# A graph network in one program: one addition and one attribute load moved to other engines, and the edge order changed

## The chip, the core and the metric

The kernel runs as one program on one core of a Trainium2 chip. The metric is the device time of one execution in microseconds (us), and for comparisons the median over several executions. The engines are TensorE (PE in the profile, with PEld for its weight loads), VectorE (DVE), ScalarE (ACT), GpSimd (POOL) and SyncE (SP). Each runs its own list of instructions in order and waits on semaphores. DMAs are issued from SP, ACT and POOL; gathers and scatters by index, and DMAs that add to their target, are issued from POOL here.

## What is computed

Two graph layers over 100,000 nodes with 64 features and 25,000 edges, sorted by destination. All is float32.

```python
h = relu(layernorm(x))
# layer 0
a = softmax over the edges of one dst of sum(h[src] * h[dst])
agg = segment_sum((h @ W_conv + b_conv)[src] * a, dst)
out = agg + relu(h @ W_res + b_res)
x2 = x + batchnorm_over_nodes(out)
# layer 1
h2 = relu(layernorm(x2))
m = gelu(gelu([h2[src], h2[dst], edge_attr] @ W_m1 + b_m1) @ W_m2 + b_m2)
boxes = segment_sum(m, dst)
c = gelu([h2, boxes] @ W_c1 + b_c1)
result = x2 + h2 + gelu(c @ W_c2 + b_c2)
```

## The kernel before

Nodes are worked on in 49 steps (S) of 128 partitions with 16 rows each, so a step's tile is 128 x 1024. Edges are worked on in 49 groups (G) of 512: 4 edges (EJ) on each of 128 partitions. The order of everything is written out by hand, as loops over pairs of steps or groups, one loop per engine. There are three stages.

The **first stage** computes layer 0 for nodes and edges at once. POOL gathers the rows of x for source and destination of every edge (8 gathers of 128 rows for a group, L587), groups in falling order. VectorE subtracts means, scales, and scans segments; TensorE transposes and multiplies; each group ends with its rows of agg, kept in SBUF. Then follow the batch norm's sums. During this stage POOL also begins to scatter agg rows to the table agg_rows in DRAM (put_agg, 4 scatters a group, L591).

The **node stage** makes x2, h2 and the result of layer 1 for all nodes as if boxes were zero. For a step s VectorE adds the normed r product to x (L937), subtracts the mean (L764, L766), sums squares (L756), inverts the deviation for two steps together (L694 to L702) and scales (L770), which gives h2 in the tile xc. POOL then adds h2 to x2 (add_h2, L637). TensorE transposes h2 (L1335) and makes both products (L1456, L1466), ScalarE the gelus, and VectorE adds the result (final_rows, L949), which SP stores. There are CS = 3 buffers of xc: x2_center of step s waits for the addition of step s - 3. In POOL's list the additions stand between the scatters of agg, and, once all 49 groups are scattered, between gathers of agg rows for the edges' sources (gather_agg, 4 a group, L587). How many groups stand in the list up to step s is `agg_groups(s)`. A gathered group goes to one of RS = 4 buffers, agg_ring, and SP stores it to edge_agg in DRAM (stash_agg, L521).

The **edge stage** corrects the rows of nodes that have edges. For a group g SP loads the edges' r product to rr[g % 6] (load_edges, L499). POOL adds the gathered agg of the source with an adding DMA from edge_agg (add_agg, L625, 128 x 256), VectorE multiplies by the batch norm's scale (scale_r, L981), and POOL adds x with another adding DMA (add_x, L631, 128 x 512). TensorE sums this with the filled agg of the destination (sum_edges, L1516 and L1519), VectorE makes h2 again (edge_x2, edge_h2), and transposes (L1530), the message products (L1540, L1542, L1549), a scan on VectorE (L1016), the last products (L1556, L1567), a transpose back (L1578) and edge_final (L1024) follow. A pair of groups is one turn of each engine's loop, in which stages of earlier groups are also worked on. SP's turn is: load_edges, load_prev (the masks for the scans), load_attr (the attributes; it waits for the message product that read the buffer before, C_m1), stash_agg. POOL's list has, for each g, add_agg(g + 2), add_x(g), the gather of a later group while there is one, and scatters of final rows (put_final, 4 a group, L591):

```python
ahead = agg_groups(S - 1) - G
last = G - ahead
...
due = min(g - 9, 2 * (g - last))
```

So no final row is scattered before group `last`, then two groups of them for every g, until they are 9 groups behind.

Edge 4p + j of a group lies on partition p in column j. After a transpose its place is column 4p + j of 512, so that in PSUM and in the weights of L1519 and L1367 every fourth column is addressed (`j:p*EJ:EJ`), 16 bytes apart.

## Time and profile before

| what | us |
|---|---|
| median of 3 executions | 1741.92 |
| their lowest and highest | 1740.9, 1746.1 |
| span of the profiled execution | 1753.3 |

The profiled execution is 11.4 us longer than the median. Its parts are: the first stage with its batch norm to about 656 us, the node stage to about 1166 us, where POOL's first add_agg stands, and the edge stage to the end. A busy engine is not always the bound, and for PE the busy time is modelled. A "wait" of 0.3 us for "issue" stands before nearly every gather and scatter of POOL and belongs to its cost.

### The profile page before, as it was taken

The numbers are of one execution on the slowest core, as the hardware profiler recorded it, in microseconds if no ns is written. First come the engines' busy times: TensorE is split into PE (matmuls) and PEld (weight loads), VectorE is DVE, ScalarE is ACT, GpSimd is POOL, SyncE is SP. The second block draws the span as 40 slices with busy tenths as digits, with TensorE's granted clock in tenths as the row PEclk, the third lists the DMA queues.
The fourth block names the chain that finished last, engine by engine and source line by source line (L and its number), as shares of the span: only waits on it lengthen the run. The fifth ranks groups of instructions, "written<-read, shape, count | busy, mean of one in ns | idle before, by whom it ended". The sixth has DMA issues, their size and how long they took to land.

```text
span 1753.3 us, 21724 instructions
## 1 busy us (share of the span) xinstructions
PE 1375.6 (78%) x6521; PEld 942.1 (54%) x6521; DVE 1361.7 (78%) x2229; ACT 833.2 (48%) x1448; POOL 1363.7 (78%) x1135
## 2 busy tenths in 40 slices
PE   3487777777776776988999889858889988787993
PEld 1266666666555564766667666634445444343541
DVE  8899899989877858898889888825767766555871
ACT  4655455545543435776668666621333432332441
POOL 7777777778777778788888887675767768888676
PEclk9788889888887877898889888955888987886987
DMA  7788776545543363444545565545656554545520
GB/s 210 249 283 290 282 264 219 165 145 157 161 150 96 106 224 102 157 166 166 201 162 186 174 200 178 160 98 108 121 120 124 118 117 97 107 89 98 122 48 18
DMA packets 154342, 273.55 MB, mean 156 GB/s; under 512 B 58386, under 2 KB 69361, under 8 KB 154228
## 3 DMA queue, kind: packets, MB, share of 16 engines
q1 hardware_dynamic: 71144, 183.91, 31.1%
q0 software_dynamic: 68112, 49.85, 16.7%
q10 hardware_dynamic: 14972, 38.41, 5.9%
q8 instruction: 54, 0.88, 0.2%
q14 instruction: 60, 0.49, 0.1%
HBM read 151.68 MB, written 121.80 MB: 156 GB/s over the span
## 4 chain that ended last, share of the span: by engine, by line
POOL 40%; issue 20%; DVE 18%; PE 13%; DMA 6%; ACT 2%; SPq 0%; POOLq 0%; DVEq 0%; ACTq 0%
POOL agg_rows L591 11%; POOL out L591 10%; POOL agg_ring L587 7%; DVE stat L756 4%; POOL xt L637 3%; DVE stat L764 3%; POOL part L587 3%; DMA rr<-edge_x 3%; DMA edge_agg<-agg_ring 2%; POOL rr L631 2%; DVE xc L770 1%; PE banks L1350 1%; DVE sums L821 1%; PE banks L1542 1%; PE banks L1540 1%
## 5 line engine op out<-in xcount | busy, mean ns | idle before, releaser
L587 POOL DMA_INDIRECT agg_ring<-agg_rows,edge_idx x196 | 233.2, 1190 | 112.2 <-DMA edge_agg<-agg_ring 57.2
L591 POOL DMA_INDIRECT agg_rows<-agg,put_first x196 | 234.0, 1194 | 55.9 <-issue 54.7
L587 POOL DMA_INDIRECT part<-in_x,edge_idx x192 | 217.3, 1132 | 58.5 <-issue 58.2
L591 POOL DMA_INDIRECT out<-agg,put_last x196 | 212.0, 1082 | 59.6 <-issue 59.6
L1335 PE MATMUL banks<-ident,xc 128*128 128x128 f32 (+1 forms) x784 | 135.1, 322 | 141.6 <-DVE xc L770 140.9
L1466 PEld LDWEIGHTS banks<-packed,cT 97*128 97x128 f32 (+1 forms) x1568 | 210.4, 218 | 45.3 <-issue 44.3
L1466 PE MATMUL banks<-packed,cT 97*128 97x64 f32 (+1 forms) x1568 | 218.6, 303 | 0.5 <-ACT cT L1198 0.5
L1335 PEld LDWEIGHTS banks<-ident,xc 128*128 128x128 f32 (+1 forms) x784 | 113.3, 177 | 152.0 <-DVE xc L770 130.8
L1456 PE MATMUL banks<-hT,packed 64*96 64x512 f32 (+1 forms) x392 | 125.5, 718 | 47.6 <-ACT cT L1198 43.0
L1081 ACT ACTIVATE hT<-banks 128x512 f32<-128x512 f32 (+1 forms) x98 | 55.4, 595 | 205.7 <-PE banks L1335 204.3
L587 POOL DMA_INDIRECT x_ring<-in_x,edge_idx x104 | 121.4, 1167 | 34.2 <-issue 34.2
L1516 PE MATMUL banks<-rr,ident 128*128 128x512 f32 (+1 forms) x98 | 69.2, 795 | 86.7 <-DMA rr<-edge_x 86.7
L587 POOL DMA_INDIRECT gout<-in_x,edge_idx x96 | 111.3, 1159 | 29.3 <-issue 29.3
L981 DVE TENSOR_TENSOR rr<-rr,bn 128x512 f32<-128x512 f32 (+1 forms) x49 | 33.9, 692 | 122.0 <-DMA rr<-edge_agg 122.0
L756 DVE TENSOR_REDUCE stat<-sq 128x16 f32<-128x1024 f32 (+1 forms) x98 | 117.1, 1212 | 14.6 <-ACT sq L1073 14.6
L1073 ACT ACTIVATE sq<-xc 128x1024 f32<-128x1024 f32 (+1 forms) x98 | 102.9, 1050 | 52.6 <-DVE xc L766 52.3
L1350 PE MATMUL banks<-hT,packed 128*128 128x512 f32 (+1 forms) x196 | 119.1, 739 | 1.3 <-ACT hT L1081 1.3
L766 DVE SCALAR_TENSOR_TENSOR xc<-stat,xt 128x1024 f32<-128x1024 f32 (+1 forms) x86 | 117.6, 1368 | 3.0
L770 DVE SCALAR_TENSOR_TENSOR xc<-xc,stat 128x1024 f32<-128x1024 f32 (+1 forms) x98 | 117.1, 1217 | 1.7
L1519 PEld LDWEIGHTS banks<-fill_b,sums 65*128 65x128 f32 (+1 forms) x392 | 99.0, 326 | 32.0 <-issue 19.1
L764 DVE TENSOR_REDUCE stat<-xt 128x16 f32<-128x1024 f32 (+1 forms) x86 | 104.1, 1210 | 14.3 <-POOL xt L637 6.1
L1257 ACT ACTIVATE sq<-banks 128x512 f32<-128x512 f32 (+1 forms) x49 | 28.9, 590 | 177.0 <-PE banks L1530 173.2
(163 smaller groups left out, 3351.2 us busy)
## 6 DMA issues: line engine op xcount, KB each, us to landing
xt<-in_x SPq DMA_DIRECT2D x84, 512.0 KB, 5.2
r_rows<-rT ACTq DMA_DIRECT2D x48, 512.0 KB, 5.4
agg_rows<-rb SPq DMA_DIRECT2D x48, 512.0 KB
out<-xt SPq DMA_DIRECT2D x36, 512.0 KB, 3.0
edge_r<-rr ACTq DMA_DIRECT2D x48, 256.0 KB, 5.0
rT<-r_rows SPq DMA_DIRECT2D x24, 512.0 KB, 6.5
part<-r_rows SPq DMA_DIRECT2D x24, 512.0 KB, 6.9
rr<-edge_r SPq DMA_DIRECT2D x48, 256.0 KB, 3.2
```

Source lines behind the costliest of these rows:

```text
L587: A.indirect_dma_start(to, None, table[:, :], bass.IndirectOffsetOnAxis(ap=idx, axis=0), bounds_check=limit, oob_is_err=False).then_inc(si ...
L591: A.indirect_dma_start(table[:, :], bass.IndirectOffsetOnAxis(ap=idx, axis=0), rows_of, None, bounds_check=limit, oob_is_err=False).then_i ...
L756: V.tensor_reduce(total, rows(squares), AX, ALU.add).then_inc(st.sem, 1)
L764: V.tensor_reduce(total, rows(source), AX, ALU.add).then_inc(st.sem, 1)
L766: V.scalar_tensor_tensor(out=rows(tile), in0=per_row(total), scalar=-1.0 / D, in1=rows(source), op0=ALU.mult, op1=ALU.add).then_inc(st.sem, 1)
L770: V.scalar_tensor_tensor(out=tile, in0=source, scalar=0.0, in1=per_row(deviation), op0=ALU.max, op1=ALU.mult).then_inc(st.sem, 1)
L1073: A.activation(sq[s % 2][0:p, :], xc[s % CS][0:p, :], ACT.Square).then_inc(st.sem, 1)
L1335: ins = T.transpose(to[:, c:c + p], xc[s % CS][0:p, c:c + P], ident[0:p, 0:p])
L1350: T.matmul(blocks(W[0][:, c], p), wres2[:, :], blocks(hT[:, c], p), start=True, stop=True)\
L1456: ins = T.matmul(blocks(bank(4 + i)[0:H2, :], p), wc1_node[i * D:i * D + D, :], blocks(hT[i * D:i * D + D, b * HALF:(b + 1) * HALF], p), s ...
L1466: ins = T.matmul(to[0:p, i * D:i * D + D], cT[b][:, i % 2, (i // 2) * P:(i // 2) * P + p], wc2[:, :], start=(i == 0), stop=(i == 7))
L1519: ins = T.matmul(to[:, j * P:(j + 1) * P], fillT[g % 2][0:D + 1, j:p * EJ:EJ], fill_b[:, :], start=False, stop=(j == EJ - 1))
```

## The change

Four things are changed.

1. In the node stage the additions of h2 to x2 for odd steps move from POOL to VectorE (add_h2_here, right after x2_center of the next even step). POOL keeps the even ones. `agg_groups` is larger, so that 83 instead of 75 groups of scatters and gathers stand in POOL's list of the node stage; `ahead` is 34 instead of 26 and `last` 15 instead of 23.
2. In the edge stage the gathered agg is loaded by SP to a ring of 4 new tiles (agg_in), and VectorE adds it in scale_r. POOL's add_agg is gone.
3. The attributes of group g + 4 are loaded by a DMA in ScalarE's list, behind the gelu of group g. SP loads only the first four.
4. Edge j * 128 + p of a group lies on partition p, column j. The index table is laid out so, and all addresses `j:p*EJ:EJ` become `j*p:(j+1)*p`.

```diff
+MI = 4
+        agg_in = [sb(f"agg_in{q}", [P, EW]) for q in range(MI)]
...
         def agg_groups(s):
-            return PUTS_AHEAD + s + 1 + (s + 1) // 6
+            return PUTS_AHEAD + 4 * (s + 1) // 3
...
+            def load_agg(g):
+                C_ra.part(sp, g - MI, 1)
+                p = edges_of(g)
+                sp.wait_ge(Y_st.of(g), Y_st.after(g))
+                sp.dma_start(agg_in[g % MI][0:p, :], edge_agg[g][0:p, :]).then_inc(C_ga.of(g), 16)
...
-                for g, do in ((a + 6, load_edges), (a + 7, load_edges), (a + 4, load_prev), (a + 5, load_prev),
-                              (a + 4, load_attr), (a + 5, load_attr)):
+                for g, do in ((a + 4, load_agg), (a + 6, load_edges), (a + 5, load_agg), (a + 7, load_edges),
+                              (a + 4, load_prev), (a + 5, load_prev)):
...
             for s in range(S):
-                add_h2(s)
+                if s % 2 == 0:
+                    add_h2(s)
...
-            for g in range(2):
-                add_agg(g)
             for g in range(G):
-                if is_group(g + 2):
-                    add_agg(g + 2)
                 add_x(g)
...
+            def add_h2_here(s):
+                p = nodes_of(s)
+                here = xb[s % XB][0:p, :]
+                B_h.done(dve, s)
+                V.tensor_tensor(here, here, xc[s % CS][0:p, :], ALU.add).then_inc(B_yv.sem, 1)
...
                 if a in pair:
                     x2_center(a)
+                if is_step(a - 1):
+                    add_h2_here(a - 1)
                 if is_step(a - 3):
                     final_rows(a - 3)
...
                 here = rows(rr[g % 6][0:p, :])
+                to = side(rr[g % 6][0:p, :], 1)
+                dve.wait_ge(C_ld.of(g), C_ld.after(g))
                 dve.wait_ge(C_ga.of(g), C_ga.after(g))
+                V.tensor_tensor(to, to, rows(agg_in[g % MI][0:p, :]), ALU.add).then_inc(C_ra.sem, 1)
+                dve.wait_ge(C_ra.sem, C_ra.after(g, 1))
                 V.tensor_tensor(here, here, cols(bn[0:p, 0, :], ER), ALU.mult).then_inc(C_ra.sem, 1)
...
                 A.activation(m1T[g % 2][0:H1, 0:c], bank(5)[0:H1, 0:c], ACT.Gelu, bias=bm1[:, :]).then_inc(C_g1.sem, 1)
+                if is_group(g + 4):
+                    load_attr(g + 4)
...
-                    ins = T.matmul(to[:, j * P:(j + 1) * P], fillT[g % 2][0:D + 1, j:p * EJ:EJ], fill_b[:, :],
+                    ins = T.matmul(to[:, j * P:(j + 1) * P], fillT[g % 2][0:D + 1, j * p:(j + 1) * p], fill_b[:, :],
...
-    idx[:, :, :G - 1] = four[:, :main].reshape(4, G - 1, P, EJ).transpose(2, 0, 1, 3)
+    idx[:, :, :G - 1] = four[:, :main].reshape(4, G - 1, EJ, P).transpose(3, 0, 1, 2)
```

POOL's list at the end of the node stage and the start of the edge stage, before (L637 is the addition of h2, L587 a gather of agg rows, L625 add_agg, L631 add_x):

```order
L637 TENSOR_TENSOR part<-part,xc 128x1024
L584 REGISTER_ALU
L587 DMA agg_ring<-agg_rows,edge_idx 128x64 x4
L584 REGISTER_ALU
L587 DMA agg_ring<-agg_rows,edge_idx 128x64 x4
L637 TENSOR_TENSOR xt<-xt,xc 106x1024
L584 REGISTER_ALU
L587 DMA agg_ring<-agg_rows,edge_idx 128x64 x4
L625 DMA rr<-edge_agg 128x4x64 x3
L631 DMA rr<-edge_x 128x512
L584 REGISTER_ALU
L587 DMA agg_ring<-agg_rows,edge_idx 128x64 x4
```

and now (L644 is the addition, L601 the gather, L638 add_x):

```order
L644 TENSOR_TENSOR part<-part,xc 128x1024
L598 REGISTER_ALU
L601 DMA agg_ring<-agg_rows,edge_idx 128x64 x4
L598 REGISTER_ALU
L601 DMA agg_ring<-agg_rows,edge_idx 128x64 x4
L598 REGISTER_ALU
L601 DMA agg_ring<-agg_rows,edge_idx 128x64 x4
L644 TENSOR_TENSOR xt<-xt,xc 106x1024
L598 REGISTER_ALU
L601 DMA agg_ring<-agg_rows,edge_idx 128x64 x4
L638 DMA rr<-edge_x 128x512
L598 REGISTER_ALU
```

Three groups stand between two additions where one or two stood, and add_x follows the last gather with no add_agg ahead of it.

SP's turn of the edge stage, before (L499 is load_edges, L426 load_prev, L505 load_attr, L521 stash_agg):

```order
L499 DMA rr<-edge_r 128x512 x2
L426 DMA xc<-prev_row 128x512 x2
L505 DMA attr<-in_edge_attr_t 32x512 x2
L521 DMA edge_agg<-agg_ring 128x256 x2
L499 DMA rr<-edge_r 128x512 x2
```

and now (L512 is load_agg, L506 load_edges, L433 load_prev, L534 stash_agg):

```order
L512 DMA agg_in<-edge_agg 128x256
L506 DMA rr<-edge_r 128x512
L512 DMA agg_in<-edge_agg 128x256
L506 DMA rr<-edge_r 128x512
L433 DMA xc<-prev_row 128x512 x2
L534 DMA edge_agg<-agg_ring 128x256 x2
```

The attribute loads, which waited for a message product, no longer stand ahead of the stores of the gathered agg.

## Rows read from the trace of the kernel before

**Rows 1.** The page: span, and the chain that ended last, by engine.

```profile
span 1753.3 us, 21724 instructions
...
POOL 40%; issue 20%; DVE 18%; PE 13%; DMA 6%; ACT 2%; SPq 0%; POOLq 0%; DVEq 0%; ACTq 0%
```

**Rows 2.** Busy time by stretch: length, then each engine's us (and instructions), clock, DMA.

```profile
0.00:606.00 606.00, 423.44 (x2126) 342.67 (x2126) 534.23 (x957) 305.06 (x603) 477.31 (x420) 0.85 0.61 200
...
678.00:1166.00 488.00, 434.54 (x2704) 323.09 (x2704) 412.64 (x503) 317.94 (x480) 402.02 (x279) 0.86 0.49 166
1166.00:1412.00 246.00, 202.07 (x640) 105.94 (x641) 163.29 (x298) 74.57 (x131) 163.01 (x144) 0.80 0.62 121
```

**Rows 3.** Waits of POOL over the whole span: total us, times, longest.

```profile
POOL agg_ring L587 <- DMA edge_agg<-agg_ring: 57.2, 9, 15.3
```

**Rows 4.** POOL's groups of instructions, 678 to 1166: busy, mean ns, idle before.

```profile
L591 POOL DMA_INDIRECT agg_rows<-agg,put_first x125 | 153.1, 1224 | 34.3 <-issue 33.7
L587 POOL DMA_INDIRECT agg_ring<-agg_rows,edge_idx x104 | 128.3, 1233 | 40.9 <-issue 27.1 <-DMA edge_agg<-agg_ring 13.1
L637 POOL TENSOR_TENSOR xt<-xt,xc 128x1024 f32<-128x1024 f32 x36 | 90.1, 2502 | 9.8 <-DVE xc L770 9.3
```

**Rows 5.** VectorE's groups of instructions, 680 to 1165.

```profile
L949 DVE TENSOR_TENSOR xt<-xt,gout 128x1024 f32<-128x1024 f32 x36 | 57.5, 1598 | 2.8 <-ACT gout L1206 2.8
...
L766 DVE SCALAR_TENSOR_TENSOR xc<-stat,xt 128x1024 f32<-128x1024 f32 x33 | 51.9, 1573 | 1.1
...
L937 DVE TENSOR_TENSOR xt<-banks,xt 128x1024 f32<-128x1024 f32 x32 | 39.0, 1218 | 12.7 <-PE banks L1438 12.7
```

**Rows 6.** POOL's groups of instructions, 1166 to 1753.

```profile
L591 POOL DMA_INDIRECT out<-agg,put_last x196 | 212.0, 1082 | 59.6 <-issue 59.6
L587 POOL DMA_INDIRECT agg_ring<-agg_rows,edge_idx x92 | 104.9, 1140 | 71.2 <-DMA edge_agg<-agg_ring 44.1 <-issue 27.1
L631 POOL DMA_DIRECT2D rr<-edge_x x49 | 68.5, 1397 | 5.4 <-DVE rr L981 5.4
L625 POOL DMA_DIRECT2D rr<-edge_agg x49 | 67.4, 1405 | 17.6 <-DMA rr<-edge_r 17.6
```

**Rows 7.** Timeline, start us and length: two message products one pair of groups apart.

```profile
1637.23 1.09 PE L1542 MATMUL banks<-sq,packed 128*80 128x512 f32 x2
...
1653.84 1.08 PE L1542 MATMUL banks<-sq,packed 128*80 128x512 f32 x2
```

**Rows 8.** Busy time in exactly that pair, columns as in rows 2.

```profile
1637.23:1653.84 16.61, 16.61 (x62) 8.72 (x61) 14.74 (x28) 7.45 (x13) 13.31 (x13) 1.00 0.66 133
```

**Rows 9.** Timeline where POOL scatters two groups for each add_x.

```profile
1489.58 2.00 PE L1542 MATMUL banks<-sq,packed 128*80 128x512 f32 x2
...
1502.53 1.40 POOL L631 DMA_DIRECT2D rr<-edge_x  x1
...
1515.69 1.40 POOL L631 DMA_DIRECT2D rr<-edge_x  x1
```

**Rows 10.** Timeline: the first scale_r, add_x of group 4, add_x of group 48.

```profile
1173.82 0.69 DVE L981 TENSOR_TENSOR rr<-rr,bn 128x512 f32<-128x512 f32 x1 [7.12 <-DMA rr<-edge_agg]
...
1205.50 1.43 POOL L631 DMA_DIRECT2D rr<-edge_x  x1
...
1683.41 1.05 POOL L631 DMA_DIRECT2D rr<-edge_x  x1
```

**Rows 11.** Timeline of TensorE: eight instructions with adjacent, then with spaced weight columns.

```profile
304.43 1.05 PE L1385 MATMUL banks<-packed,heT 128*128 128x128 f32 x8
...
305.54 1.87 PE L1367 MATMUL banks<-packed,sums 65*128 65x65 f32 x8
...
307.24 0.60 PE L1358 MATMUL banks<-ident,weighted 128*65 128x128 f32 x4
```

**Rows 12.** Mean ns by line: a transpose with spaced, one with adjacent PSUM columns.

```profile
L1504 PE MATMUL banks<-ident,agg 128*64 128x128 f32 x192 | 37.6, 331 | 0.0
L1376 PE MATMUL banks<-ident,part 128*128 128x128 f32 x192 | 37.0, 327 | 3.3 <-DVE part L770 3.3
```

More of the change, by code:

```diff
@@ L281, in program @@
         B_h = stage("h2_ready")
-        B_y = stage("h2_added_to_x2")
+        B_y = stage("h2_added_on_gpsimd")
+        B_yv = stage("h2_added_on_vector")
         B_t = stage("h2_transposed", 2)
@@ L292, in program @@
         C_ld = Slots(E_st.sems, before=G)
-        C_ga = slots("gathered_agg_added", 4)
+        C_ga = slots("gathered_agg_loaded", MI)
         C_x = slots("edge_x_added", 4)
@@ L298, in program @@
         C_fs = stage("agg_filled")
-        C_ra = stage("edge_r_scaled")
+        C_ra = stage("edge_r_scaled", 2)
         C_as = stage("edge_x2_summed")
@@ L513, in load_prev @@
                     sp.wait_ge(B_t.sem, B_t.after(S - 1))
-                    sp.wait_ge(B_y.sem, B_y.after(S - 1))
+                    h2_added(sp, S - 1)
+                    h2_added(sp, S - 2)
                 load_same(mask[g % MS], prev_row, g, g, 0, P, C_sm)
@@ L542, in _ @@
                             load_attr(g)
+                            load_agg(g)
                         load_edges(g)
@@ L619, in gather_agg @@
                     gather(agg_ring[g % RS][0:p, j * D:(j + 1) * D], agg_rows, idx_of(src_idx, g, j, p), G_a.of(g))
-            def add_agg(g):
-                p = edges_of(g)
-                pool.wait_ge(C_ld.of(g), C_ld.after(g))
-                pool.wait_ge(Y_st.of(g), Y_st.after(g))
-                A.dma_start(side(rr[g % 6][0:p, :], 1), rows(edge_agg[g][0:p, :]), accum_op=ALU.add)\
-                 .then_inc(C_ga.of(g), 16)
             def add_x(g):
@@ L947, in final_rows @@
                 dve.wait_ge(B_og.sem, B_og.after(s))
-                dve.wait_ge(B_y.sem, B_y.after(s))
+                h2_added(dve, s)
                 V.tensor_tensor(here, here, gout[s % 2][0:p, :], ALU.add).then_inc(B_fin.sem, 1)
@@ L1262, in copy_dst_x2, with load_attr @@
                 A.activation(rows(agg_of(g, p)), side(bank(1 + g % 2)[0:p, :], 0), ACT.Copy).then_inc(C_xd.sem, 1)
+            def load_attr(g):
+                C_m1.done(act, g - 4)
+                c = edges_of(g) * EJ
+                q = (g % 4) * DE
+                A.dma_start(attr[q:q + DE, 0:c], eaT[:, g * EG:g * EG + c]).then_inc(C_ea.of(g), 16)
             def edge_gelu1(g):
@@ L1670, in edge_layout @@
     main = (G - 1) * EG
-    idx[:, :, :G - 1] = four[:, :main].reshape(4, G - 1, P, EJ).transpose(2, 0, 1, 3)
-    rest = four[:, main:E].reshape(4, -1, EJ)
-    idx[:rest.shape[1], :, G - 1] = rest.transpose(1, 0, 2)
+    idx[:, :, :G - 1] = four[:, :main].reshape(4, G - 1, EJ, P).transpose(3, 0, 1, 2)
+    rest = four[:, main:E].reshape(4, EJ, -1)
+    idx[:rest.shape[2], :, G - 1] = rest.transpose(2, 0, 1)
     windows = np.stack([pad[k:E + k].reshape(FP, FC) for k in range(3)], axis=1)
```

16 lines of the change are left out of this document (9 added, 7 removed).

## The prediction, made blind

> **What bounds the kernel now.** I read the chain that ended last first [rows 1]: POOL and the "issue" gaps, which are mostly POOL's 0.3 us ahead of each gather or scatter, make 60% of it. No engine is far behind, so the question is the same in each stage: which list is never idle?
>
> In the first stage VectorE is busy 534 of 606 us, POOL 477 plus 0.3 us for each of its 420 instructions, together about 600 [rows 2]. POOL is gapless, and the stage ends with its last gathers.
>
> In the node stage POOL has 229 indirect DMAs. With the gap ahead of each they take (153.1 + 34.3 + 128.3 + 27.1) / 229 = 1.50 us each [rows 4]. 228 of them, with 49 additions of 2.5 us, make 342 + 122 = 464 of 488 us. The other 24 us are its waits, 13.1 for the agg ring and about 10 for h2 [rows 4]. So POOL's list sets this stage, but VectorE (413) and TensorE (435) stand close behind it [rows 2].
>
> In the edge stage the length goes by pairs of groups. From add_x of group 4 to that of group 48 there are 22 pairs in 1683.4 - 1205.5 = 477.9 us, 21.7 each [rows 10]. A clean pair takes 16.61 us, with TensorE busy all of it and VectorE 14.74 [rows 7, 8]. The difference comes from two things. While POOL still gathers, it stands 57.2 us in 9 waits, 44.1 of it here, for the store that frees a buffer of agg_ring [rows 3, 6]. SP issues this store behind the attribute load, which waits for a message product. Later POOL scatters two groups for each add_x, and two add_x are 1515.69 - 1502.53 = 13.2 us apart, 26.3 a pair [rows 9]. After the last add_x come 1753.3 - 1683.4 = 69.9 us, in which POOL has 44 scatters of 1.39 left [rows 6]: 61 us, so the tail is POOL's as well.
>
> **First stage: 1 us less.** Only the addresses change. TensorE loads weights for L1367 from spaced columns. Eight instructions take 1.87 us, and eight of L1385 with adjacent ones 1.05 [rows 11], so 0.8 us a group go. POOL and VectorE set this stage and TensorE waits for them, so this shows only for the last groups, behind the last gather. I take 1 us (0 to 3).
>
> **Node stage: 7 us less.** POOL's list changes from 228 indirect DMAs and 49 additions to 260 and 25: 390 + 62 = 452 us, 12 less. VectorE gets 24 additions. Both inputs lie in SBUF, as in L949, which without a stretch takes as long as L937, 1.22 us: 29 us. But L949 and L766 are stretched to 1.60 and 1.57 [rows 5], and the candidates for it are POOL's additions. (0.38 + 0.35) x 48 = 35 us for 49 additions are 0.71 each, and 24 of them go: 17 back. VectorE's net 12 us fit into the 75 us that it is idle. In the other direction, POOL's indirect DMAs take 1.22 to 1.23 us here [rows 4] and 1.08 where fewer large VectorE operations run [rows 6]. 0.14 x 228 = 32 us over 147 such VectorE operations are 0.22 each, so 24 more cost POOL 5. That leaves 7. Bounds: 20 less, if its waits shrink too; 12 more, if VectorE's net addition lies wholly on the path. In VectorE's list x2_center of the next odd step and two final additions are queued behind add_h2_here. It waits for nothing there, since h2 is VectorE's own result of the turn before.
>
> The Trainium skill (GPSIMD Engine Reference, Key points) says that GpSimd shares its SBUF interfaces with VectorE and is disturbed by VectorE instructions with two SBUF inputs; by it, the new additions in either stage would cost POOL time, as the 5 us above do.
>
> **Start of the edge stage: 9 us less.** The first scale_r waits 7.1 us for the adding DMA of POOL [rows 10], which stands behind POOL's last gathers. Now agg_in is loaded while the node stage runs, and scale_r follows the last final addition at once: 7 less. The first groups also come sooner by one DMA issue of 1.4 us each on POOL; two of these I count, 2 us.
>
> **The 22 pairs: 85 us less.** Each engine's need for a pair:
>
> - TensorE: 16.6 in the clean pair, less 2 x 0.8 for the weights of L1519: 15.0.
> - VectorE: 14.74 and two additions of 128 x 256. Half of the 0.69 that 128 x 512 takes [rows 10] to two thirds of it, 0.45: 15.6. The clean pair has 1.9 us in which VectorE waits for ScalarE's squares or for its own last result. The new work can fill little of that, so 17.2. Ends: 16.6 (all of it filled) and 19.2 (2 us of new waiting).
> - POOL while it gathers: 8 x 1.43 + 2 x (1.40 + 0.3) = 14.9. Without add_agg it loses 2 x 1.4 us and its waits for rr. With one group of scatters for each g: 8 x 1.39 + 3.4 = 14.5.
>
> So VectorE takes POOL's place as the bound, with 17.2. The stall on agg_ring goes: stash_agg now stands behind loads that wait for sum_edges and message_scan of earlier turns, a pair ahead of the product that it waited for. What is late next is POOL's double scattering. From `last` = 15 on, 2 * (g - last) overtakes g - 9 after six groups, where it took 14 before. In these three pairs POOL needs 16 x 1.39 + 3.4 = 25.6. It falls behind by 3 x (25.6 - 17.2) = 25 us. TensorE wants an add_x only in the next pair, so a part is absorbed. I take 15 (0 to 25).
>
> Sum: 22 x 17.2 + 15 = 393, against 478: 85 less. The DMAs of the attributes cost ScalarE an issue and no more, since it is busy 7.5 of 16.6 us [rows 8]. The tail of 69.9 us stays, since as many scatters are left behind the last add_x.
>
> On addresses, the two transposes that write PSUM with 16 bytes between columns (L1504) or without (L1376) take 331 and 327 ns [rows 12], so I count nothing for those. The Trainium skill (SBUF — State Buffer, Door 1: The DMA port swizzle) has two rules here. Any non-contiguous access to PSUM significantly slows matmuls, so the transposes would get faster, on an engine that no longer bounds. And a stride of four fp32 in SBUF is free, so L1519 would gain nothing and TensorE would stay at 16.6 a pair, below 17.2, with the same sum. Rows 11 and 12 disagree with both.
>
> **The sum.** 1 + 7 + 9 + 85 = 102 us off the profiled execution's 1753.3: 1651. That execution is 11.4 us above the median, and I take the same difference from the median: 1741.9 - 102 = 1640.
>
> **The rivals.**
>
> *Waits remain in the pairs.* VectorE, TensorE and ScalarE hand over to each other several times a pair, and the clean pair shows this loop only with TensorE as its pace. If VectorE as the pace leaves 19.2 a pair, the pairs take 22 x 19.2 + 15 = 437, 41 less instead of 85: 1684. For it: the many waits for ScalarE; a low clock in places has the same effect. Against: a clean pair appears wherever POOL keeps up. Chance 0.22.
>
> *All goes well.* Pairs at 16.6, the double scattering absorbed, and the node stage 20 shorter: 113 + 20 + 9 + 3 = 145 less, 1597. Near this, below 1605: 0.08.
>
> *TensorE's clock falls, and it ends slower.* In the clean pair the clock is 2.4 GHz (1.00) [rows 8]. At 1.2 GHz the two passes of L1542 take 2.00 instead of 1.09 us [rows 7, 9]. Once TensorE waits for VectorE in every pair, as it waits in the stretches with 0.80 [rows 2], it might be given the low level for most of the stage. At the low level a pair needs 15.0 x 1.8 = 27. This decides if the pair passes 21.7 + 17/22 = 22.5, that is if TensorE spends over 60% of its work at 1.2 GHz; at 85% the pair is 25.2 and the time 1742 + 77 - 17 = 1802. Against: a TensorE that has become the bound doesn't idle, and the dense stretch has the full clock. Chance 0.04.
>
> *The change doesn't do what it says.* agg_in could come late, because load_agg stands in SP's list between load_edges, which wait for sum_edges; then one DMA wait is only replaced by another, and with pairs of 21.7 the time is 1742 - 7, or within 0.3% if the node stage gives nothing. SP reaches it a pair early, so 0.04 together, 0.03 of it within 0.3%.
>
> **How the numbers follow.** The forecast, 1605 to 1665, has 0.62, the rivals 0.22, 0.08, 0.04 and 0.04. The range 1605 to 1695 leaves out the last two, the best case and the upper end of the first rival. Faster by over 0.3% (5 us, about what a measurement of this kernel can tell from no change): 0.93; within it 0.03; slower 0.04.
>
> **What would show it.** VectorE's wait ahead of scale_r, and POOL's for agg_ring in the edge stage, near zero; add_x of groups 4 to 48 in about 393 us; three pairs of about 25 from group 16; L1519 and L1367 at about 1.05 us for eight at full clock; L949's mean below 1.5; first add_x about 7 us sooner after the last node rows. I am wrong if VectorE is idle over 3 us a pair in the edge stage, if the node stage gets longer, or if the granted clock there falls below 0.7.

## The result, and the profile after

| | us |
|---|---|
| median before, 4 executions | 1741.7 (1740.9 to 1746.1) |
| median after, 4 executions | 1619.6 (1614.9 to 1620.4) |
| ratio, 95% interval | 0.9295 (0.9271 to 0.9318) |
| predicted | 1640 (1605 to 1695) |

It is faster by 122 us, 20 more than predicted, and inside the range. The profiled executions lie further apart than the medians: 1753.3 before, 11.4 above its median [rows 1], 1613.1 after, 6.5 below its own. So the terms below add up to 140 us, and 18 of them are scatter between executions. This scatter favoured the forecast: between the two profiled executions the miss is 38 us, between the medians 20.

The page of the changed kernel, span and chain by engine; [rows 1] had POOL at 40%:

```profile
span 1613.1 us, 21823 instructions
...
POOL 31%; DVE 28%; issue 19%; PE 13%; DMA 4%; ACT 3%; DVEq 0%; SPq 0%; POOLq 0%; ACTq 0%
```

The stages can be laid beside each other by four marks: POOL's first and last addition of h2, and its add_x of groups 4 and 48. From the timeline of after (start us, length):

```profile
675.95 2.35 POOL L644 TENSOR_TENSOR xt<-xt,xc 128x1024 f32<-128x1024 f32 x1
...
1148.72 2.36 POOL L644 TENSOR_TENSOR xt<-xt,xc 106x1024 f32<-106x1024 f32 x1
...
1191.35 1.02 POOL L638 DMA_DIRECT2D rr<-edge_x  x1
...
1544.10 1.00 POOL L638 DMA_DIRECT2D rr<-edge_x  x1 [1.08 <-DVE rr L997]
```

and the first two marks in before (its last two are in [rows 10]):

```profile
678.34 2.38 POOL L637 TENSOR_TENSOR xt<-xt,xc 128x1024 f32<-128x1024 f32 x1
...
1158.12 2.36 POOL L637 TENSOR_TENSOR xt<-xt,xc 106x1024 f32<-106x1024 f32 x1
```

| stretch | before | after | difference | predicted |
|---|---|---|---|---|
| to the first addition of h2 | 678.3 | 676.0 | -2.4 | -1 |
| to the last (node stage) | 479.8 | 472.8 | -7.0 | -7 |
| to the add_x of group 4 | 47.4 | 42.6 | -4.8 | -9 |
| to the add_x of group 48, 22 pairs | 477.9 | 352.8 | -125.1 | -85 |
| tail | 69.9 | 69.0 | -0.9 | 0 |

Nearly the whole of the surprise is in the pairs. The two message products one pair apart, and busy time in exactly that pair and in a longer stretch of the steady part (columns as in [rows 2]; [rows 7, 8] are before's):

```profile
1412.36 1.08 PE L1566 MATMUL banks<-sq,packed 128*80 128x512 f32 x2
...
1428.36 1.08 PE L1566 MATMUL banks<-sq,packed 128*80 128x512 f32 x2
```

```profile
1412.36:1428.36 16.00, 15.09 (x61) 6.62 (x61) 15.32 (x30) 7.45 (x13) 11.51 (x11) 1.00 0.55 143
...
1364.00:1544.00 180.00, 169.62 (x672) 74.18 (x672) 172.48 (x326) 84.39 (x149) 133.74 (x119) 1.00 0.56 135
```

A steady pair is 16.0 us, not 17.2. VectorE is busy 15.32 of it, and over 180 us 96%; TensorE has 15.09. VectorE is the pace, as forecast. Two of POOL's waits over the whole execution, which answer [rows 3]:

```profile
POOL rr L638 <- DVE rr L997: 32.6, 22, 7.1
POOL agg_ring L601 <- DMA edge_agg<-agg_ring: 21.8, 8, 7.9
```

POOL now waits for VectorE's scale_r. Of the 21.8 us for the ring, 17.0 lie in the node stage and only 4.8 in the edge stage, where there were 44.1 [rows 6]. The double scattering is still there. POOL's three pairs from add_x 16 take 23.4, 24.9 and 23.7 us, as forecast (about 25), and two pairs at the message products 20.6 and 23.5 us:

```profile
1304.83 1.08 PE L1566 MATMUL banks<-sq,packed 128*80 128x512 f32 x2
...
1325.44 1.08 PE L1566 MATMUL banks<-sq,packed 128*80 128x512 f32 x2
...
1348.89 1.09 PE L1566 MATMUL banks<-sq,packed 128*80 128x512 f32 x2
```

### The profile page after: what moved, and what is told of

The parts are those of the page before. It is cut to its first block, busy times and chain, and to the rows that moved or that the text cites. A ratio compares the mean times of both kernels' runs of the same rounds, so it can differ in the third digit from the quotient of the medians.

```text
span 1613.1 us, 21823 instructions
## 1 busy us (share of the span) xinstructions
PE 1254.2 (78%) x6521; PEld 842.9 (52%) x6521; DVE 1376.9 (85%) x2302; ACT 832.7 (52%) x1448; POOL 1250.2 (78%) x1062
## 2 busy tenths in 40 slices
DMA packets 132612, 273.54 MB, mean 170 GB/s; under 512 B 30404, under 2 KB 47658, under 8 KB 132496
## 4 chain that ended last, share of the span: by engine, by line
POOL 31%; DVE 28%; issue 19%; PE 13%; DMA 4%; ACT 3%; DVEq 0%; SPq 0%; POOLq 0%; ACTq 0%
POOL agg_rows L605 12%; POOL part L601 6%; DVE stat L760 4%; DVE stat L768 4%; POOL out L605 4%; PE banks L1490 3%; POOL agg_ring L601 3%; DVE sq L1032 3%; DVE part L774 2%; DVE sums L1006 2%; POOL gout L601 2%; POOL x_ring L601 2%; DMA edge_agg<-agg_ring 2%; PE banks L1480 2%; PE banks L1374 2%
## 5 line engine op out<-in xcount | busy, mean ns | idle before, releaser
L601 POOL DMA_INDIRECT agg_ring<-agg_rows,edge_idx x196 | 233.7, 1192 | 82.8 <-issue 55.9
L605 POOL DMA_INDIRECT out<-agg,put_last x196 | 221.7, 1131 | 59.8 <-issue 59.5
L601 POOL DMA_INDIRECT part<-in_x,edge_idx x192 | 218.9, 1140 | 58.5 <-issue 57.6
L1490 PEld LDWEIGHTS banks<-packed,cT 97*128 97x128 f32 (+1 forms) x1568 | 214.7, 222 | 42.6 <-issue 42.4
L1490 PE MATMUL banks<-packed,cT 97*128 97x64 f32 (+1 forms) x1568 | 223.0, 307 | 0.0
L601 POOL DMA_INDIRECT x_ring<-in_x,edge_idx x104 | 122.0, 1173 | 34.3 <-issue 34.0
L601 POOL DMA_INDIRECT gout<-in_x,edge_idx x96 | 109.1, 1137 | 29.3 <-issue 28.7
L760 DVE TENSOR_REDUCE stat<-sq 128x16 f32<-128x1024 f32 (+1 forms) x98 | 117.2, 1212 | 16.6 <-ACT sq L1089 16.6
L768 DVE TENSOR_REDUCE stat<-xt 128x16 f32<-128x1024 f32 (+1 forms) x86 | 104.1, 1210 | 19.6 <-POOL xt L644 14.6
L770 DVE SCALAR_TENSOR_TENSOR xc<-stat,xt 128x1024 f32<-128x1024 f32 (+1 forms) x86 | 111.9, 1302 | 2.9
L1213 ACT ACTIVATE cT<-banks,packed 96x512 f32<-96x512 f32 (+1 forms) x98 | 66.8, 681 | 71.8 <-PE banks L1480 71.6
L1382 PE MATMUL banks<-ident,weighted 128*65 128x128 f32 (+1 forms) x196 | 36.7, 321 | 75.0 <-DVE weighted L815 75.0
L1222 ACT ACTIVATE gout<-banks 128x512 f32<-128x512 f32 (+1 forms) x98 | 57.7, 589 | 59.9 <-PE banks L1490 59.9
L1127 ACT ACTIVATE esq<-part 128x512 f32<-128x512 f32 (+1 forms) x98 | 61.2, 625 | 48.6 <-DVE part L770 48.6
```

Source lines behind the costliest of these rows:

```text
L601: A.indirect_dma_start(to, None, table[:, :], bass.IndirectOffsetOnAxis(ap=idx, axis=0), bounds_check=limit, oob_is_err=False).then_inc(si ...
L605: A.indirect_dma_start(table[:, :], bass.IndirectOffsetOnAxis(ap=idx, axis=0), rows_of, None, bounds_check=limit, oob_is_err=False).then_i ...
L760: V.tensor_reduce(total, rows(squares), AX, ALU.add).then_inc(st.sem, 1)
L768: V.tensor_reduce(total, rows(source), AX, ALU.add).then_inc(st.sem, 1)
L770: V.scalar_tensor_tensor(out=rows(tile), in0=per_row(total), scalar=-1.0 / D, in1=rows(source), op0=ALU.mult, op1=ALU.add).then_inc(st.sem, 1)
L1213: A.activation(blocks(cT[b][0:H2, 0, :], p), blocks(bank(4)[0:H2, :], p), ACT.Gelu, bias=bc1[:, :])
```

## Experiments on one part at a time

The first four kernels ran on one chip beside before, which took 1743.2 us there (median of 7). They are compared with after's 1619.6.

**Part 2 taken back.** GpSimd adds the gathered agg again; VectorE only scales. The other parts of the change stay.

```diff
-                            load_agg(g)
...
-                V.tensor_tensor(to, to, rows(agg_in[g % MI][0:p, :]), ALU.add).then_inc(C_ra.sem, 1)
...
+                if is_group(g + 2):
+                    add_agg(g + 2)
                 add_x(g)
```

> The changed kernel with one part undone: POOL adds the gathered agg again with an adding DMA, and VectorE has no addition in scale_r. The rest stays (fewer gathers in the edge stage, attributes from ScalarE, new edge order). Theory: VectorE paces the clean pairs of the changed kernel at 16.0 us, but POOL needs 2 x 1.4 us more a pair, about 17.3 while it gathers and 16.9 to 17.3 with one group of scatters, and 28 in the three pairs with two groups. So the pairs come out at about 17.3, which is 22 x 1.3 + 8 = 37 us more than the changed kernel, plus 5 for the first scale_r: 1660. Rival (the adding DMA was never the cost, only the ring stalls were): VectorE loses 0.9 us of work a pair and the time stays within 8 us of 1620.

Measured: 1638.8 us (1635.8 to 1640.6), 0.940 of before (0.937 to 0.943). That is 19 more than after, half of what the theory said. GpSimd, 124 us of the steady part, its groups and then all engines:

```profile
L598 POOL DMA_INDIRECT out<-agg,put_last x65 | 66.7, 1026 | 19.7 <-issue 19.7
L638 POOL DMA_DIRECT2D rr<-edge_x x17 | 24.2, 1422 | 0.0
L632 POOL DMA_DIRECT2D rr<-edge_agg x16 | 23.6, 1475 | 0.0
```

```profile
1436.00:1560.00 124.00, 123.76 (x489) 53.65 (x488) 114.86 (x215) 62.29 (x110) 104.60 (x98) 1.00 0.70 134
```

GpSimd is busy for 104.6 us of the 124, and 19.7 us of issue gaps fill it up; a pair takes 15.06. TensorE is filled too, 123.76 of 124 us at full clock, and 15.06 is also the 15.1 us that its work of a pair takes. So GpSimd keeps up here, and which of the two sets the pair the trace doesn't part. It is faster than after's 16.0, where VectorE is the pace: in this part of the edge stage moving the addition cost 0.9 us a pair. It pays elsewhere, by the time that the two adding DMAs take in GpSimd's list. They overlap in the profile:

```profile
1519.62 1.33 POOL L632 DMA_DIRECT2D rr<-edge_agg  x1
1520.46 1.39 POOL L638 DMA_DIRECT2D rr<-edge_x  x1
```

That is 2.2 us for both, not the sum of their lengths, and only the 1.0 of add_x is left in after: 1.2 us less for each group. The way from add_x 4 to 48 is 369.2 us against 352.8. To group 16, while GpSimd still gathers, it is 5.3 us longer; in the six steps with two groups of scatters, 13.1 to 14.6 us each for 11.5 to 13.0, it is 9.5 longer. Behind them it is 1.6 longer in all: the shorter steady pairs only make up for a late one at the end (20.5 us). The way from the last addition of h2 to add_x 4 is 4.4 us longer (47.0 against 42.6), so the gain at the start of the edge stage belongs to this part.

**Part 3 taken back.** SP loads the attributes, at the end of its turn ahead of the stash, as before the change. Part 2 stays, so SP has load_agg as well.

```diff
             def load_attr(g):
+                C_m1.done(sp, g - 4)
...
-                              (a + 4, load_prev), (a + 5, load_prev)):
+                              (a + 4, load_prev), (a + 5, load_prev), (a + 4, load_attr), (a + 5, load_attr)):
...
-                if is_group(g + 4):
-                    load_attr(g + 4)
```

> The changed kernel with one part undone: SP loads the attributes again, at the end of its turn and ahead of the stores of gathered agg. Theory: the store that frees agg_ring and load_agg come one pair later again. While POOL gathers (15 groups, 7 pairs) this costs about 6 us every second pair, 15 to 25 us; in the rest SP loads agg_in for group a + 4 only after the message product of group a + 1, and scale_r of a + 4 would wait for it: 1 to 4 us a pair more in 15 pairs. Together 30 to 60 us more: 1650 to 1680. Rival: the loads are early enough anyway and only the ring stall returns: 10 to 20 us more, 1630 to 1640.

Measured: 1792.3 us (1788.3 to 1794.7), 1.027 of before (1.023 to 1.030). Both expectations missed by over 110 us. This kernel is slower than before, and the waits tell why (total us, times, longest), of SP's own list, of VectorE and of POOL:

```profile
SPq L518 <- PE banks L1559: 474.1, 45, 19.5
```

```profile
DVE rr L996 <- DMA agg_in<-edge_agg: 190.6, 22, 14.9
```

```profile
POOL rr L639 <- DVE rr L998: 151.7, 28, 12.5
POOL agg_ring L602 <- DMA edge_agg<-agg_ring: 72.6, 13, 18.2
```

SP stands at load_attr until the message product (L1559 here) has read the old attributes. The agg_in load of the next turn is queued behind that. I read these waits so: the product of one pair releases SP, SP starts agg_in, VectorE adds it, and only then can the next products come, a closed loop of 24 us a pair. In before the wait was there too, 427.7 us, but behind it stood only loads with a lead of two turns and the stash. With SP's turn in this order, part 3 is a precondition of part 2.

**Part 3 alone, put into before.**

```diff
-                              (a + 4, load_attr), (a + 5, load_attr)):
+                              ):
...
+                if is_group(g + 4):
+                    load_attr(g + 4)
```

> The kernel before with one part of the change alone: the attributes of group g + 4 are loaded from ScalarE's list. Theory: SP's stores of gathered agg come a pair earlier, and the 44 us of waits for agg_ring in the edge stage and the 18 for rr go. In the part with gathers POOL then needs 8 x 1.43 + 2 x 3.1 = 17.7 a pair instead of about 20.4, over 11 pairs 30 us; the part with two scattered groups for each g stays at 26.3 a pair. Time 1742 - 30 to 45 = 1697 to 1712. Rival: the ring stalls only took the place of waits for TensorE, 0 to 10 us less.

Measured: 1693.9 us (1693.6 to 1695.6), 0.972 of before (0.968 to 0.975). So this one edit brings 49 us of the 122, a little more than the 30 to 45 expected. POOL's wait for the ring:

```profile
POOL agg_ring L586 <- DMA edge_agg<-agg_ring: 13.4, 5, 7.9
```

against 57.2 [rows 3], 44 us less. The pairs while POOL gathers are 16.6 us; while it scatters twice they stay at 26.3.

**Part 4 taken back.** Edge 4p + j lies on partition p again.

```diff
-T.matmul(to[:, j * P:(j + 1) * P], fillT[g % 2][0:D + 1, j * p:(j + 1) * p], fill_b[:, :],
+T.matmul(to[:, j * P:(j + 1) * P], fillT[g % 2][0:D + 1, j:p * EJ:EJ], fill_b[:, :],
```

and so in the other five places and in the index tables.

> The changed kernel with one part undone: edge 4p + j on partition p again, with columns 16 bytes apart in PSUM and in the weights. Theory: VectorE paces a pair at 16.0, TensorE needs 15.1 and with the old weight loads 16.6 to 16.8. So TensorE becomes the bound by 0.6 to 0.8 us a pair, 13 to 18 us, and the last groups of the first stage cost 1 to 3: 14 to 20 us more, 1634 to 1640. Rival, by my prediction, in which VectorE needed 17.2: no change, within 5 us of 1620.

Measured: 1640.6 us (1630.0 to 1645.5), 0.940 of before (0.935 to 0.945), 21 more than after. TensorE's message products in its steady part:

```profile
1417.35 1.09 PE L1566 MATMUL banks<-sq,packed 128*80 128x512 f32 x2
...
1433.95 1.09 PE L1566 MATMUL banks<-sq,packed 128*80 128x512 f32 x2
```

The pair is 16.61 us, the same as the clean pair of before [rows 7]: TensorE bounds it, at full clock, and VectorE's two additions are hidden. The way from add_x 4 to 48 is 370.0 us, 17 of the 21. The sum of parts: 49 us for part 3 alone, 19 for part 2 and 21 for part 4 when each is the last to come. The remaining 33 show in none of these four runs. Part 1, the moved additions of h2 with the larger table, wasn't taken back here, and the rest is what the parts bring only together; such a sum needn't close, since part 3 was measured without the others and they with it.

**VectorE's time, made longer.** A dummy addition of 128 x 256, read by nobody, goes in behind each scale_r; the outputs are unchanged. This run and the next three had another chip, on which before takes 1948.7 us (median of 11, 1899.2 to 1970.1; the section on the hardware says what is other there). In the next experiment, whose edge stage is that of after, steady pairs take 16.0 us there too, so the edge stage can be compared between the chips; whole times only within one.

```diff
+                C_ra.done(dve, g - 1)
+                V.tensor_tensor(prod[:, :], packed[:, 0:EW], packed[:, EW:2 * EW], ALU.add).then_inc(C_ra.sem, 1)
```

> The kernel after with one dummy VectorE addition (128x256, its result read by nobody) put into each group of the edge stage, behind scale_r. In the steady pair of after VectorE is busy 15.32 us of 16.0 and has no wait that its trace shows. Theory (VectorE alone sets the pair, and every us of work on it counts in full): two additions of 0.42 us and their gaps make the steady pair 16.9 us; over 22 pairs, 4 or 5 of them set by the scatters of two groups a turn, 17 x 0.9 = 15 to 20 us, so 1635 to 1640. Rival (VectorE still waits for others somewhere in the pair, and fills that time): pair 16.0 to 16.3, 1620 to 1627.

Measured: from add_x 4 to 48 371.2 us. The kernel of the next experiment took 353.0 on this chip: 18.2 more, as the theory said. (Whole time: 1869.9, 1856.4 to 1880.9; the numbers near 1635 were for the first chip.) Two pairs of its steady part:

```profile
1697.73:1731.86 34.13, 31.87 (x121) 14.09 (x120) 32.35 (x63) 14.89 (x26) 20.93 (x20) 0.95 0.53 130
```

A pair is 17.06 us with VectorE busy 16.18: 0.86 more work, 1.06 more time, idle 0.88 a pair where after has 0.68. VectorE's list is the pace. TensorE's granted clock was 0.95 in this window, where it was 1.00 in after's, and whether the other 0.2 us come from that the run doesn't show.

**h2 all on GpSimd.** The order of the indirect DMAs stays as in after.

```diff
-                if s % 2 == 0:
-                    add_h2(s)
+                add_h2(s)
...
-                if is_step(a - 1):
-                    add_h2_here(a - 1)
```

> The kernel after with all 49 additions of h2 on GpSimd again; the number of indirect DMAs in the node stage (83 groups), and all of the edge stage, as in after. Theory (what the node stage of before was short of is GpSimd's time, and VectorE's additions buy it): 24 additions of 2.50 us return to an engine that is busy 382 us of the 481 from first to last addition, and they hold up the chain x2 to h2 to relu, so the node stage grows by 20 to 55 us: 1640 to 1675. Rival (GpSimd has 99 us to spare there and the additions run in it): 1612 to 1628.

Measured: 1841.7 us (1836.5 to 1868.5); the kernel with the spread scatters below, which has half of these additions on VectorE, took 1837.6. The node stages, this kernel first, then the other:

```profile
858.00:1372.00 514.00, 449.31 (x2688) 332.17 (x2688) 419.88 (x507) 321.03 (x481) 422.10 (x305) 0.83 0.49 162
```

```profile
853.00:1369.00 516.00, 446.19 (x2638) 331.61 (x2640) 415.03 (x529) 318.74 (x473) 374.62 (x280) 0.82 0.49 160
```

GpSimd does 47 us more in the same time. Its waits for VectorE in either, this kernel's first:

```profile
POOL xt L644 <- DVE xc L773: 106.9, 3, 104.7
...
POOL part L644 <- DVE xc L773: 1.1, 1, 1.1
```

```profile
POOL xt L644 <- DVE xc L774: 26.6, 6, 9.6
POOL part L644 <- DVE xc L774: 20.9, 4, 6.6
```

The 104.7 us are the wait ahead of the stage's first addition, which isn't in the other kernel's list: that one is taken from 858 us on, behind its first addition; without it this kernel waits 3.3 us and goes through, where the other waits 47.5. So on this chip the rival holds. This list has no slack left, though: 422.1 us busy, 69.8 of issue gaps, 17.4 of waits for DMAs and the 3.3 make 513 of 514 us. In the first trace of after GpSimd has no such wait: 376.4 us busy, 72.4 of issue gaps and 22.0 of waits for DMAs make 471 of the 473 us. I ran it once more beside after, to see it on a chip like the first:

> The kernel after with all 49 additions of h2 on GpSimd. On the other chip its node stage took 513.5 us, GpSimd going through it without a gap (422 us busy, 70 of issue, 20 of waits for DMAs), and the kernels with half of the additions took 516 to 519 with GpSimd waiting 47 us for VectorE. In the first trace of after GpSimd has no such wait and needs 473 us (376 busy, 72 issue, 22 for DMAs). Theory (on a chip where the node stage runs as in that trace GpSimd sets it, and the moved additions are worth their time): 513 us against 473, so 35 to 40 us slower than after, 1655 to 1660. Rival (the stage is set by TensorE's clock, as on the other chip, and where the additions stand is worth nothing): within 5 us of after.

> The kernel after, unchanged, beside the three others. The runs with dummy additions, with all h2 on GpSimd, with fewer indirects and with spread scatters were timed on a chip where the kernel before takes 1948.7 us, not 1742, so what they cost or gain can be read only stage by stage; this is the missing ratio. Expected: 0.930 of before and 353 us from the add_x of group 4 to that of group 48 if the chip is like the first one; if it is like the other, about 0.948 of before and the same 353 us, since the run with all h2 on GpSimd, whose edge stage is that of after, showed 353.0 there.

But that chip was like the second (before 1988.7 us, 1961.2 to 2005.8). This kernel took 1892.3 us (1858.5 to 1911.6), after 1898.0 (1843.6 to 1910.3), 0.954 of before by the medians and 0.940 by the lowest of each. Four executions that scatter by 3% show no difference between this kernel and after. The node stage took 521.1 and 544.1 us in profiled executions 40 and 49 us above the lowest of their kernels. From add_x 4 to 48 the same code took 355.2 and 359.8 us there, where two other traces had 352.8 and 353.0; why, I can't explain. What the move of h2 is worth on the first chip stays open. The sum of GpSimd's list says up to 40 us; no run shows it.

**Fewer indirects in the node stage.** The table of the node stage is that of before (75 groups, not 83).

```diff
-            return PUTS_AHEAD + 4 * (s + 1) // 3
+            return PUTS_AHEAD + s + 1 + (s + 1) // 6
```

> The kernel after with the old table of the node stage: 75 groups of indirect DMAs beside the additions of h2, not 83, so 8 groups (32 DMAs) go back to the edge stage and its scatters begin at group 23, not 15. Theory (GpSimd doesn't set the node stage any more, TensorE and VectorE do, so taking 40 us of work from it gives little, and the edge stage has too few scatter turns left): node stage shorter by 5 to 20 us, edge stage longer by 15 to 35 us, since two groups a turn last longer; 1628 to 1645. Rival (the node stage is still set by GpSimd, so its 32 x 1.24 = 40 us return there, and the edge stage hides them): node stage -30 to -40, edge stage +0 to +10, 1585 to 1600.

Measured: 1855.8 us (1849.1 to 1869.6). The kernel with all of h2 on GpSimd, 14 us below it, is the nearest on this chip with the larger table, and after itself didn't run there. The node stage is 492.7 us, 24 to 27 shorter than in the two kernels there whose node stage is that of after (516.5 and 519.5), and the way from add_x 4 to 48 is 390.8, 38 longer than the 353.0. The theory had the direction of both, and both are somewhat larger than it said (5 to 20 and 15 to 35). 14 add_x in a row have two groups of scatters between them, and five pairs take 23.6 to 26.8 us. The rival had hoped for 30 to 40 us in the node stage and for a cover in the edge stage. An indirect DMA costs 0.8 us in the node stage (25 / 32), and 1.2 where it is left to the edge stage (38 / 32), so the larger table is a gain, of some 13 us by these two stretches. That the stage gets shorter at all, though GpSimd waits 47.5 us for VectorE in the kernel with the larger table, no run explains.

**The scatters spread.** One number of after.

```diff
-                due = min(g - 9, 2 * (g - last))
+                due = min(g - 9, 6 * (g - last) // 5)
```

> The kernel after with one number changed: put_final begins at the same group 15 but takes 6 groups in 5 turns, not 2 a turn until it has caught up, so no turn but every fifth has two. In after two pairs there took 20.6 and 23.5 us for 16.0. By the groups of GpSimd in a steady pair (8 indirects of 1.17 us with 0.3 us of issue each, 2 additions of 0.97) a pair with 2.4 groups needs 14.8 us, under VectorE's 16.0. Theory: the bump goes and nothing takes its place, -9 to -12 us, 1608 to 1611. Rival (the scatters are then late at the end and are waited for there, or slow every fifth turn): within 4 us of after, or up to 5 slower, 1616 to 1625.

> The kernel after with put_final taking 6 groups in 5 turns, beside after on one chip: on the other chip the way from the add_x of group 4 to that of group 48 took 344.0 us, 9 less than the 353 of after's code there. Expected now 344 and 9 to 10 us less than after in the median (0.5 to 0.6%); a rival is that the tail behind group 48 takes the gain back, then less than 4.

Measured: the way from add_x 4 to 48 takes 344.0 us the first time and 343.7 the second, against 353.0 and 352.8 for after's edge stage. All pairs from group 4 to 42 are 16.0 to 16.7 us in both; the bump is gone. The first and the last mark on the second chip:

```profile
1423.39 1.02 POOL L638 DMA_DIRECT2D rr<-edge_x  x1
...
1767.43 1.04 POOL L638 DMA_DIRECT2D rr<-edge_x  x1
```

The whole times are 1837.6 us (1823.2 to 1859.5), 0.943 of before's median there, and 1855.0 (1850.3 to 1884.9), 0.937 of before (0.925 to 0.949), where after took 1898.0 (1843.6 to 1910.3), its lowest below all of these. The tail behind add_x 48 is 71.0 and 75.4 us, for after's 69.0 and 69.4. So the 9 us are seen twice between the two marks; in whole times they are smaller than the scatter of these chips, and a gain over after isn't established.

**The additions of agg split.** On top of the spread scatters, from group 18 on GpSimd adds agg for odd groups and VectorE for even ones.

```diff
+def by_pool(g):
+    return g >= 18 and g % 2 == 1
...
+                if is_group(g + 2) and by_pool(g + 2):
+                    add_agg(g + 2)
                 add_x(g)
```

> The kernel after with the scatters spread (6 groups in 5 turns from group 15) and, from group 18 on, the gathered agg of every odd group added by GpSimd's adding DMA, that of the even ones still by VectorE. A pair then costs VectorE 15.6 us (16.0 less one addition of 0.42), GpSimd 14.8 on average with 2.4 groups of scatters and one more adding DMA of 1.0 + 0.3, so 16.1 where a pair has 12 indirects and 13.6 where it has 8. Theory (VectorE and TensorE set the pair, each by its own sum of work; TensorE needs 15.1): 12 to 15 pairs of 15.5 to 15.7, so 5 us less than with the scatters spread alone, 14 less than after. Rival (GpSimd's turns with two groups of scatters set the pace of every fifth turn and what is won in the others is lost there): within 3 us of the spread scatters alone, or up to 10 slower.

Measured: 1889.8 us (1888.2 to 1894.0), 0.956 of before (0.946 to 0.965), and 363.2 us from add_x 4 to 48, 19 more than with the spread scatters alone. The theory fell, and the rival named the place but not the size. Message products of its steady part:

```profile
1660.92 1.08 PE L1592 MATMUL banks<-sq,packed 128*80 128x512 f32 x2
...
1685.39 1.08 PE L1592 MATMUL banks<-sq,packed 128*80 128x512 f32 x2
...
1700.22 1.08 PE L1592 MATMUL banks<-sq,packed 128*80 128x512 f32 x2
```

One pair takes 24.5, the next 14.8. GpSimd's groups from 1645 to 1800 fill the window, with 26.1 us of issue:

```profile
L617 POOL DMA_INDIRECT out<-agg,put_last x86 | 101.9, 1184 | 26.1 <-issue 26.1
L657 POOL DMA_DIRECT2D rr<-edge_x x17 | 20.9, 1232 | 0.0
L651 POOL DMA_DIRECT2D rr<-edge_agg x9 | 12.1, 1349 | 0.0
```

My 14.8 us for an average pair was too low even without the adding DMA: 9.6 x (1.17 + 0.3) + 2 x 0.97 = 16.1, and in the trace of the spread scatters GpSimd used 15.4 of 16.0 (124.6 us busy and 29.1 of issue gaps in 160). With the adding DMA one of the two groups takes 2.25 us for both DMAs, and GpSimd needs 9.6 x (1.18 + 0.30) + 2.25 + 1.0 = 17.5 us. The way from add_x 20 to 40 is 17.5 us a pair. The list that had been relieved became the bound again.

## Why the prediction was right

**What bounds.** In the edge stage VectorE takes GpSimd's place: right, and shown by the dummy additions, since each us of VectorE's work there costs about a us. That GpSimd's list sets the first two stages fits its trace, where it has hardly a gap, but no run tests it for the first stage, and for the node stage the one test that told something, on the second chip, went to the rival.

**First stage, 1 us: 2.4**, inside 0 to 3, but not by the cause that was named. The kernel before with part 3 alone, which keeps the old addresses, has its first addition of h2 at 675.9 us, and after with the old addresses at 676.7, where the three kernels with the new ones have 675.8 to 676.4. So the addresses show next to nothing here, and the 2.4 us are for the most part scatter of before's profiled execution.

**Node stage, 7 us: 7.0.** That it agrees so well is luck. The same node stage as in before, in the kernel with part 3 alone, lasts from the first to the last of these:

```profile
675.92 2.37 POOL L636 TENSOR_TENSOR xt<-xt,xc 128x1024 f32<-128x1024 f32 x1
...
1151.77 2.36 POOL L636 TENSOR_TENSOR xt<-xt,xc 106x1024 f32<-106x1024 f32 x1
```

475.9 us, not 479.8. That of after takes 472.8, and 473.3, 475.6 and 475.3 with one of the other parts taken back. By these six traces the change brings 0.3 to 7 us here, with 32 more indirect DMAs done in the stage; GpSimd's list itself (busy and issue) went from 454 to 449 us. The stretch of VectorE by GpSimd's additions went as worked out. The rows of after that answer [rows 5]:

```profile
L959 DVE TENSOR_TENSOR xt<-xt,gout 128x1024 f32<-128x1024 f32 x36 | 48.1, 1336 | 0.0
L770 DVE SCALAR_TENSOR_TENSOR xc<-stat,xt 128x1024 f32<-128x1024 f32 (+1 forms) x34 | 47.5, 1398 | 1.2
```

1598 became 1336 and 1573 became 1398 ns. GpSimd's indirect DMAs took 1241 and 1237 ns for 1224 and 1233 [rows 4], 3 us in all where I had said 5.

**Start of the edge stage, 9 us: 4.8.** The wait of 7.1 us [rows 10] is gone, and VectorE adds and scales at once:

```profile
1158.49 1.23 DVE L959 TENSOR_TENSOR xt<-xt,gout 106x1024 f32<-106x1024 f32 x1 [10.83 <-ACT gout L1222]
1159.63 0.42 DVE L995 TENSOR_TENSOR rr<-rr,agg_in 128x256 f32<-128x256 f32 x1
1160.08 0.69 DVE L997 TENSOR_TENSOR rr<-rr,bn 128x512 f32<-128x512 f32 x1
```

But what ends last there is the last final_rows, which waits 10.8 us for ScalarE; the gathers behind the last h2 were no longer what the first scale_r stood behind. The 2 us for an issue less on POOL were 0.4: from add_x 0 to 4 it took 30.7 us before and 30.3 after.

**The 22 pairs, 85 us: 125.** This is the term that was mis-sized. TensorE's need of 15.0 us is 15.1. For VectorE I had 15.6 of work, and it has 15.3. The step that failed is the idle time: of 1.9 us in the clean pair I let the new work fill only 0.3, because VectorE waits there for ScalarE's squares. The end "16.6 (all of it filled)" was the nearest, and even that kept TensorE's old pace. Those waits were slack and no loop: once VectorE had more to do and TensorE less, its idle time shrank to 0.7 us. 22 x (17.2 - 16.0) = 26 us. The double scattering costs 4.6 + 7.5 = 12 us for 15. The other 11 come from the measure more than from the work: I had put 22 pairs at the pace of VectorE between two add_x, but add_x needn't keep that pace. After the start POOL runs ahead, with four pairs of 13.1, 12.5, 12.8 and 13.7 us, and at the message product the same 22 pairs take 361.7 us,

```profile
1193.72 1.08 PE L1566 MATMUL banks<-sq,packed 128*80 128x512 f32 x2
...
1555.38 1.09 PE L1566 MATMUL banks<-sq,packed 128*80 128x512 f32 x2
```

and 352.8 at add_x: 9 of the 11. Together 26 + 3 + 11 = 40. Of these 40 some belong to before's profiled execution, which was long: the medians are only 20 us off in all.

**The stall on agg_ring**, and the reason given (the stash behind the attribute load), is shown by part 3 put into before: 44 of 57 us of the wait went. What the prediction didn't see is how much hung on it: with the attribute load still in SP's list, part 2 alone costs more than it brings. The rival on SP's order ("agg_in could come late") had 0.04 and took load_edges for the cause; with part 3 in the change it didn't happen, and without it the pair is 24 us, not before's 21.7.

**Addresses.** Weight loads from spaced and from adjacent columns, before and after:

```profile
L1519 PEld LDWEIGHTS banks<-fill_b,sums 65*128 65x128 f32 (+1 forms) x392 | 99.0, 326 | 32.0 <-issue 19.1 <-DVE sums L990 9.2
```

```profile
L1543 PEld LDWEIGHTS banks<-fill_b,sums 65*128 65x128 f32 (+1 forms) x392 | 53.3, 202 | 51.6 <-DVE sums L1006 36.4 <-issue 15.2
```

326 ns became 202, and taking it back gave a pair of 16.6 instead of 16.0. That run took the PSUM addresses back as well, but its transposes into spaced columns take 292 ns (L1528, 196 of them) for after's 287, while its weight loads take 324 for 202: the weights are the cause. The Trainium skill (SBUF — State Buffer, Door 1: The DMA port swizzle) gives four fp32 as how far one can stride for free, and the sentence before says that each access that crosses to a new 16-byte line pays. Columns 16 bytes apart cross with each, and the runs agree with that sentence: for these loads the stride isn't free. The prediction had gone by the rows.

**The tail, 0 us: 0.9. The clock** stayed at 2.4 GHz (1.00) in the steady part, and its rival (0.04) didn't come. **The sum**: 102 predicted, 122 in the medians.

## What to carry to other kernels

When one engine sets the pace of a pair, the waits of the next busiest are not lost time by themselves: ask if they lie on a loop that closes within the pair. If they don't, new work fills them, and here the pace was the largest sum of work plus 4 to 5 per cent. A load that waits for a late product must not stand ahead of loads that others wait for; whoever adds a load to a queue counts what it is queued behind. And when work is moved off an engine, look for where that engine was really the pace: here the moved addition pays at the start, while POOL gathers, and in the turns with two scatters, and costs 0.9 us a pair in the steady ones.

## What the runs showed of the hardware

**An uneven set of DMA engines, most likely.** On the second and third chip before took 12 and 14% longer than on the first, and after, which ran on the third, 17%. The time is lost in the first two stages: the first addition of h2 comes at 851 to 904 us instead of 676, and the edge stage of after's code is as long as on the first chip, or up to 7 us longer. In a stretch of 46 us of the first stage, in 40 slices, on the second chip:

```profile
DMA  9999971110011011214992111110111111110111
GB/s 413 413 426 403 399 291 45 27 34 11 21 29 29 0 29 29 29 29 110 365 246 52 29 29 29 27 27 11 21 29 29 29 29 29 29 21 7 29 29 29
```

With a busy share over 90% it is 399 to 426 GB/s. Then for up to 20 us it is mostly 29, with a busy share of a tenth: by my estimate, 426 / 16 = 27, about what one of 16 engines would move. The chain on the page of that profile has 13% for "another core or an unknown queue" there, which the first chip's doesn't show. It reads as if one DMA engine lags and everything waits for its share of each transfer. The views don't part the engines, so this is a reading, not shown.

**Adding DMAs with small pieces.** Without the adding DMA to half of each row of rr, the packets under 512 bytes fell from 58,386 to 30,404 (pages of the profile, before and after), and the mean length of the add_x that stayed fell from 1397 ns [rows 6] to 985:

```profile
L605 POOL DMA_INDIRECT out<-agg,put_last x196 | 221.7, 1131 | 59.8 <-issue 59.5 <-DVE agg L1040 0.3
...
L638 POOL DMA_DIRECT2D rr<-edge_x x48 | 47.3, 985 | 27.7 <-DVE rr L997 27.7
```

It is 1422 ns in the steady part of the kernel where part 2 is taken back, and 1232 where half of the groups have it, that is about 1.4 us with and 1.0 without an adding DMA right ahead. The two overlap by 0.5 us in the profile, so the 0.4 us aren't a cost on top: both together take GpSimd 2.25 us, one alone 1.0, and the one that is gone in after saves 1.25.

**GpSimd beside VectorE.** The scatters of the edge stage take 1131 ns in after and took 1082 before [rows 6]. With part 2 taken back they take 1026 in 124 us of the steady part, where after has 1167 (1364 to 1544 us). The Trainium skill (GPSIMD Engine Reference, Key points) says that VectorE's instructions with two SBUF inputs disturb GpSimd, and the direction agrees; the spread scatters had 1101 with the same additions, on the second chip, so it is not the whole of it.
